# TensorE's inflows of a state-space scan, two states at a time in 64x128 tiles, with other steps left to VectorE

## The reference

```python
u, z = split(x @ in_w.T, 2)               # 256 channels each
u = silu(causal_conv(u))                  # 4 taps
dbc = u @ xproj_w.T                       # 64 for dt, 16 for B, 16 for C
dt = softplus(dbc[..., :64] @ dt_w.T + dt_b)
dA = exp(dt[..., None] * A)               # 16 states n
dBu = (dt * u)[..., None] * Bm[:, :, None, :]
h = dA_t * h + dBu_t                      # over the tokens t, for each channel and state
y = einsum('bdn,bn->bd', h, C_t) + u * D
out = y * silu(z) @ out_w.T
```

## Time and profile before

| | |
|---|---|
| median of 3 runs | 1566.91 us (1558.56 to 1570.34) |
| the profiled execution | 1558.44 us, span 1556.6 |
| Mamba stage in it | from about 10 to 975 us, a unit of it 58 |
| busy over the whole span | TensorE 87%, VectorE 75%, GpSimd 68%, ScalarE 62% |
| granted TensorE clock | 0.975 of full, 1.00 in most of the stage |
| chain that ended last | TensorE 52%, ScalarE 15%, VectorE 15%, GpSimd 5% |

### The profile page before, as it was taken

How to read it: one execution, slowest core, us unless ns; L and a number is a source line. 1 busy time by engine, 2 the same in 40 slices (tenths; PEclk the granted TensorE clock), 3 DMA queues, 4 the chain that set the end, 5 groups by cost and what they waited for, 6 DMA issues and landing times.

```text
span 1556.6 us, 43543 instructions
## 1 busy us (share of the span) xinstructions
PE 1347.9 (87%) x17914; PEld 1014.4 (65%) x17914; DVE 1161.2 (75%) x1926; ACT 958.4 (62%) x1750; POOL 1060.3 (68%) x684
## 2 busy tenths in 40 slices
PE   6798888889889989889889777898998999997595
PEld 3566766656756666666666666457997666666594
DVE  6788888888898887888888886523335888876376
ACT  6877777777766776876876765313555555542144
POOL 3798888888898888888888886340333466583552
PEclk9899999999999999999999989999999999999798
DMA  5122232232232222222222220531124200001223
GB/s 189 58 93 95 85 107 81 85 108 80 85 103 80 91 102 80 91 102 80 95 98 79 97 91 29 213 98 36 52 79 126 98 1 2 2 29 54 80 64 98
DMA packets 51604, 128.95 MB, mean 83 GB/s; under 512 B 8080, under 2 KB 33168, under 8 KB 41696
## 3 DMA queue, kind: packets, MB, share of 16 engines
q1 hardware_dynamic: 46640, 116.36, 21.8%
q0 software_dynamic: 4768, 9.81, 1.9%
HBM read 113.20 MB, written 18.56 MB: 85 GB/s over the span
## 4 chain that ended last, share of the span: by engine, by line
PE 52%; ACT 15%; DVE 15%; issue 8%; POOL 5%; another core or an unknown queue 2%; DMA 1%; SPq 1%; DVEq 0%; ACTq 0%; POOLq 0%
PE py L530 8%; PE pa L508 8%; DVE hh L925 5%; ACT da L723 4%; POOL hc L1077 3%; PE pr L1990 2%; PE bank L1536 2%; PE bank L1532 2%; PE bank L1546 2%; PE pq L413 2%; PE pq L385 2%; PE pr L2004 2%; ACT uz L625 2%; DVE hh L902 2%; PE pr L2193 2%
## 5 line engine op out<-in xcount | busy, mean ns | idle before, releaser
L1077 POOL TENSOR_TENSOR hc<-hh,cs 128x1024 f32<-128x1024 f32 x256 | 602.9, 2363 | 138.5 <-DVE hh L925 70.6
L925 DVE TENSOR_TENSOR_SCAN hh<-da,st,pa 128x512 f32<-128x512 f32 x240 | 293.6, 1266 | 65.5 <-PE pa L508 55.5
L508 PEld LDWEIGHTS pa<-dg,dtut 64*64 64x64 f32 x10240 | 180.8, 137 | 179.4 <-issue 175.6
L530 PE MATMUL py<-ident,hc 128*128 128x128 f32 x2048 | 277.1, 279 | 19.3 <-ACT yt L743 19.2
L508 PE MATMUL pa<-dg,dtut 64*64 64x64 f32 x10240 | 219.1, 226 | 80.9 <-DVE yz L934 38.5
L530 PEld LDWEIGHTS py<-ident,hc 128*128 128x128 f32 x2048 | 227.8, 142 | 44.7 <-ACT yt L743 21.2
L723 ACT ACTIVATE da<-dt,w 128x512 f32<-128x512 f32 x320 | 212.7, 711 | 11.3 <-DVE hh L925 10.4
L723 ACT ACTIVATE pa<-dt,w 128x512 f32<-128x512 f32 x192 | 127.7, 684 | 97.2 <-DVE hh L925 96.4
L925 DVE TENSOR_TENSOR_SCAN hh<-pa,st,hh 128x512 f32<-128x512 f32 x144 | 175.4, 1267 | 2.6 <-ACT pa L723 1.9
L385 PE MATMUL pq<-xn,w 128*128 128x512 f32 x248 | 121.0, 613 | 5.0 <-ACT xn L759 3.6
L925 DVE TENSOR_TENSOR_SCAN hh<-da,pa 128x512 f32<-128x512 f32 x80 | 93.2, 1207 | 29.4 <-PE pa L508 26.3
(11 more groups left out here) (349 smaller groups left out, 2807.8 us busy)
## 6 DMA issues: line engine op xcount, KB each, us to landing
cs<-bcrows SPq DMA_DIRECT2D x64, 1024.0 KB, 4.7
bs<-bcrows SPq DMA_DIRECT2D x32, 256.0 KB, 3.9
xsorted<-in_pads SPq DMA_DIRECT2D x13, 387.0 KB, 5.3
rot<-in_rot SPq DMA_DIRECT2D x4, 1024.0 KB, 5.0
wx<-in_l_w SPq DMA_DIRECT2D x4, 1024.0 KB, 10.3
ysort<-ytoken SPq DMA_DIRECT2D x14, 256.0 KB
wx<-in_l_w SPq DMA_DIRECT2D x1, 3072.0 KB, 12.3
wx<-in_l_w SPq DMA_DIRECT2D x1, 2304.0 KB, 16.7
```

Of the source, the lines that this page charges most:

```text
L508: i = pe.matmul(pa[turn["step", s, h] % SLOTS][c * HQ:(c + 1) * HQ, kt * P + r * HQ:kt * P + (r + 1) * HQ], dtut[rows, kt, h * P + c * HQ: ...
L530: i = pe.matmul(py[:, h * CH + kt * P:h * CH + (kt + 1) * P], hc[s % HCS][:, h, t], ident[:, :], is_transpose=True, start=n == 0 and kt == ...
L925: v.tensor_tensor_scan(hh[s % HHS][:, h, :], a, b, 0.0 if first else st[:, m % 2, n, h:h + 1], ALU.mult, ALU.add).then_inc(s_taken, 1)
L1077: g.tensor_tensor(hc[s % HCS][:, :, :], hh[s % HHS][:, :, :], cs[j % 2][:, s % CG, :].unsqueeze(1).broadcast_to([P, HF, CH]), ALU.mult).th ...
```

## The change

- `BY_G` is gone: GpSimd makes no inflow, the B rows are no longer loaded for it. `BY_V` becomes (6, 7, 12, 13), and TensorE has twelve steps: 0 to 5, 8 to 11, 14, 15.
- TensorE's steps go in pairs of states. The first step of a pair makes the inflows of both states for half 0, the second for half 1. VectorE scans accordingly two states for one half, and GpSimd's `times_c` and `keep_state` of either state wait for the second step; `keep_state` is done two steps later instead of one.
- An inflow is one block of 8 matmuls in 64x128 tiles: 64 tokens by 128 channels stationary, a diagonal of 64 for each of two states moving (128 columns). Rows 0 to 63 of the array write one bank of a pair, rows 64 to 127 the other. The two states are interleaved element by element over the pair, and the 128-token blocks by fours of tokens; a scan reads every second element of both banks. For that, `turn_b` and `turn_dtu` take every fourth token.
- A bank that held such an inflow is free only when both scans of its pair have read it (`free`).
- The order on TensorE changes: the inflow of step s + 1 first, then the spread, then `add_up`; in n = 10 it comes last.

```diff
-BY_G = (0, 12)
-BY_V = (1, 6, 11, 13)
-BY_P = tuple(n for n in range(NS) if n not in BY_G + BY_V)
+BY_V = (6, 7, 12, 13)
+BY_P = tuple(n for n in range(NS) if n not in BY_V)
...
-                pa = [bank(k, f"pa{i}") for i in range(SLOTS)]
+                pa2 = [bank(k, f"pa{i}", 2) for i in range(SLOTS // 2)]
+                pa = [pa2[i // 2][:, i % 2 * CH:(i % 2 + 1) * CH] for i in range(SLOTS)]
...
-                        order += [("step", s, h) for h in range(HF)]
+                        if n in BY_P:
+                            order += [("flow", pair_of(s), BY_P.index(n) % 2, j) for j in range(2)]
+                        else:
+                            order += [("step", s, h) for h in range(HF)]
...
+                def free(i):
+
+                    i -= SLOTS
+                    return i // 2 * 2 + 2 if handed_items[i][0] == "flow" else i + 1
+
+                def scanned(s):
+
+                    k = s % NS
+                    return (turn["flow", pair_of(s), HF - 1, BY_P.index(k) % 2] if k in BY_P else turn["step", s, HF - 1]) + 1
...
+                def by_fours(t):
+
+                    return t.rearrange("p (j k) -> p k j", k=4)
...
-                            i = pe.transpose(pb[:, kt * P:(kt + 1) * P], dtu[m % 2][:, h, kt * P:(kt + 1) * P], ident[:, :])
+                            i = pe.transpose(pb[:, kt * P:(kt + 1) * P], by_fours(dtu[m % 2][:, h, :])[:, kt, :], ident[:, :])
...
+                    def inflow(s):
+
+                        m, k, h = s // NS, pair_of(s), BY_P.index(s % NS) % 2
+                        i = turn["flow", k, h, 0]
+                        pe.wait_ge(s_turnk, turned_count(m, 2))
+                        pe.wait_ge(s_dg, k + 1)
+                        if i >= SLOTS:
+                            pe.wait_ge(s_taken, free(i + 1))
                         for kt in range(4):
                             for r in range(2):
-                                h, rows = (r + phase) % 2, slice(r * HQ, (r + 1) * HQ)
-                                for c in range(2):
-                                    i = pe.matmul(pa[turn["step", s, h] % SLOTS][c * HQ:(c + 1) * HQ, kt * P + r * HQ:kt * P + (r + 1) * HQ],
-                                                  dtut[rows, kt, h * P + c * HQ:h * P + (c + 1) * HQ], dg[pair % DGS][rows, of, kt, :],
-                                                  start=True, stop=True)
-                        i.then_inc(s_pin, 1)
+                                rows = slice(r * HQ, (r + 1) * HQ)
+                                mm = pe.matmul(pa[i % SLOTS + r].rearrange("p (j k n) -> p k n j", n=2, k=4)[:, kt, :, :],
+                                               dtut[rows, kt, h * P:(h + 1) * P], dg[k % DGS][rows, :, kt, :], start=True, stop=True)
+                        mm.then_inc(s_pin, 1)
...
-                        spreads = s + 2 < STEPS and by_vector(s + 2)
-                        if spreads and n != LAG:
+                        if s + 1 < STEPS and by_pe(s + 1) and n != 10:
+                            inflow(s + 1)
+                        if s + 2 < STEPS and by_vector(s + 2):
                             spread_b(s + 2)
...
-                        if flows:
-                            inflow(s + 1, 0)
...
                         if n != LAG and s >= LAG:
                             add_up(s - LAG)
-                        if flows:
-                            inflow(s + 1, 1)
...
                         prep(m + 1, n)
+                        if n == 10:
+                            inflow(s + 1)
...
+                        if by_pe(s):
+                            k, h = pair_of(s), BY_P.index(n) % 2
+                            for j in range(2):
+                                q = 4 * k + 2 * h + j
+                                if q >= DAS:
+                                    k0, j0 = (q - DAS) // 4, (q - DAS) % 4
+                                    act.wait_ge(s_taken, turn["flow", k0, j0 // 2, j0 % 2] + 1)
...
-                        if s >= 1:
-                            keep_state(s - 1)
+                        if s >= 2:
+                            keep_state(s - 2)
...
+                        if by_pe(s):
+                            k, h = pair_of(s), BY_P.index(n) % 2
+                            own = PAIRS[k % len(PAIRS)]
+                            if h == 0 and NS * m + own[1] >= HHS:
+                                v.wait_ge(s_hc, NS * m + own[1] - HHS + 1)
+                                v.wait_ge(s_st, kept_states(NS * m + own[1] - HHS))
+                            v.wait_ge(s_pin, 2 * k + h + 1)
+                            for j, nj in enumerate(own):
+                                i, q = turn["flow", k, h, j], 4 * k + 2 * h + j
+                                v.wait_ge(s_slot, slot_count(i))
+                                inflows = pa2[i // 2 % (SLOTS // 2)][:, j::2]
+                                v.tensor_tensor_scan(hh[(NS * m + nj) % HHS][:, h, :], da[q % DAS][:, :], inflows,
+                                                     0.0 if first else st[:, m % 2, nj, h:h + 1], ALU.mult, ALU.add).then_inc(s_taken, 1)
```

More of the change, by code:

```diff
@@ L217, in layer0_mamba @@
             s_crow, s_cout = sem("bc_rows_kept"), sem("bc_rows_out")
-            s_cin, s_bin = [sem(f"c_in{i}") for i in range(2)], sem("b_in")
+            s_cin = [sem(f"c_in{i}") for i in range(2)]
             s_hc, s_st = sem("hc_made"), sem("state_kept")
@@ L747, in keep_state @@
                             return
-                        act.wait_ge(s_taken, turn["step", s, HF - 1] + 1)
+                        act.wait_ge(s_taken, scanned(s))
                         act.activation(st[:, s // NS % 2, s % NS, :], hh[s % HHS][:, :, CH - 1], ACT.Identity).then_inc(s_st, 1)
@@ L918, in scan @@
                             v.wait_ge(s_st, kept_states(NS * (m - 1) - 1))
-                        for h in range(HF):
-                            i = turn["step", s, h]
-                            v.wait_ge(s_slot, slot_count(i))
-                            a, b = pa[i % SLOTS][:, :], hh[s % HHS][:, h, :]
-                            if by_pe(s):
-                                a, b = da[2 * (before(BY_P, s) % 2) + h][:, :], pa[i % SLOTS][:, :]
-                            v.tensor_tensor_scan(hh[s % HHS][:, h, :], a, b,
-                                                 0.0 if first else st[:, m % 2, n, h:h + 1], ALU.mult, ALU.add).then_inc(s_taken, 1)
+                        if by_pe(s):
[11 more added lines that the diff above has]
+                                                     0.0 if first else st[:, m % 2, nj, h:h + 1], ALU.mult, ALU.add).then_inc(s_taken, 1)
+                        else:
+                            v.wait_ge(s_db, made(BY_V, s))
+                            for h in range(HF):
+                                i = turn["step", s, h]
+                                v.wait_ge(s_slot, slot_count(i))
+                                v.tensor_tensor_scan(hh[s % HHS][:, h, :], pa[i % SLOTS][:, :], hh[s % HHS][:, h, :],
+                                                     0.0 if first else st[:, m % 2, n, h:h + 1], ALU.mult, ALU.add).then_inc(s_taken, 1)
                     def gate(m):
@@ L1063, in b_diagonals @@
                         if k >= DGS:
-                            m0, last = (k - DGS) // len(PAIRS), PAIRS[(k - DGS) % len(PAIRS)][-1]
-                            g.wait_ge(s_pin, 2 * before(BY_P, NS * m0 + last) + 2)
-                        columns = bt[m % 2][:, :, own[0]:own[-1] + 1:own[-1] - own[0]].rearrange("p t n -> p n t")
+                            g.wait_ge(s_pin, 2 * (k - DGS) + 2)
+                        columns = bt[m % 2][:, :, own[0]:own[1] + 1].rearrange("p t n -> p n t")
                         g.tensor_tensor(dg[k % DGS][:, :, :, :], eye2[:, :].unsqueeze(1).unsqueeze(1).broadcast_to([P, 2, 4, HQ]),
@@ L1070, in times_c @@
                     def times_c(s):
-                        g.wait_ge(s_taken, turn["step", s, HF - 1] + 1)
+                        g.wait_ge(s_taken, scanned(s))
                         j = s // CG
@@ L1086, in mamba_gpsimd @@
                     g.wait_ge(s_small, 96)
-                    inflow(0)
-                    b_diagonals(0)
+                    for k in range(2):
+                        b_diagonals(k)
                     for s in range(STEPS):
@@ L1092, in mamba_gpsimd @@
                             dt_times_u(m + 1)
-                        if s + 2 < STEPS and (s + 2) % NS in BY_G:
-                            inflow(s + 2)
-                        ahead = [k for k in range(1, UNITS * len(PAIRS)) if NS * (k // len(PAIRS)) + PAIRS[k % len(PAIRS)][0] == s + 4]
+                        ahead = [k for k in range(2, UNITS * len(PAIRS)) if NS * (k // len(PAIRS)) + PAIRS[k % len(PAIRS)][0] == s + 4]
                         for k in ahead:
```

91 lines of the change are left out of this document (25 added, 66 removed).

## The result

The changed kernel takes 1614.35 us (1611.34 to 1618.21), the kernel before 1563.87 beside it (four runs, one more than before the forecast): ratio 1.032, 95% interval 1.027 to 1.037. The forecast was 1585. So the sign was right and the size was not: +50 us instead of +18.

A forecast was written before the change was run, and what follows sets the result against it. Handovers bound each unit: TensorE's queue in pieces 1, 2 and 4, VectorE in piece 3. 0.9 + 0.35 + 1.13 - 1.1 = +1.28 us a unit, +18 us in all, on the median 1566.9 gives 1585; range 1545 to 1615.

The forecast's parts named there:

- The mechanism: State-space stage: no engine is full; handovers set a unit's length, TensorE's queue in three pieces, VectorE in the other.
- piece 1: From the scan of step 0 to the end of the gate: 19.8 us before, forecast +0.9 through TensorE's queue.
- piece 3: From the first `factor` to the scan of step 13: 9.5 us before, forecast +1.13 for one more VectorE inflow.
- Piece 4: From the scan of step 13 to the next unit's scan 0: 11.1 us before, forecast 10.0, so -1.1.
- The block: TensorE's 8 matmuls in two passes for a whole step's inflow: taken as 1.05 us from three estimates, 1.02 to 1.09.
- Estimate (a): Price of a TensorE block as twice an old phase plus the switch of tile shape: 1.09 us.
- the price of 0.15 for entering: TensorE's `add_up` ahead of an inflow takes 1.03 us against 0.87 ahead of anything else, so entering costs 0.15 more.
- Piece 2: From the end of the gate to the first `factor`: 17.5 us before, forecast 17.8, so +0.35.
- the strided output: Rival: blocks writing columns 32 bytes apart double the column time, a block 1.92 us, 1715 in all; chance 0.10.
- the dtu transposes: Rival: transposes reading every fourth element of dtu take twice 0.5 us a group, +15 us, 1600; chance 0.13.
- the switches: Rival: TensorE's row tiles lose the 0.3 us tile-shape switches, saving 45 us, 1540; chance 0.14, half for a part.
- nothing: Rival: the bare wait and the extra inflow are worth as much as the queue gains, 1567; chance 0.16.

The follow-up runs named there:

- no_dd: Changed kernel without the 16 matmul instructions a unit that add u * D to y: ratio 1.0225 to the kernel before.
- fill_uz3: Changed kernel with four unread 512-column matmuls a unit added in TensorE's pauses and three `uz` tiles instead of two: ratio 1.019 to the kernel before.
- fill: Changed kernel with four 512-column matmuls a unit, whose products nobody reads, added in TensorE's pauses: ratio 1.023 to the kernel before.
- flat_out: Changed kernel with each matmul of a block writing its 128 columns to adjacent places instead of 32 bytes apart: ratio 1.035 to the kernel before.
- v1: Changed kernel with one of VectorE's four inflows moved from step 7 to step 1: ratio 1.006 to the kernel before.
- uz3: Changed kernel with three `uz` tiles instead of two: ratio 1.0385 to the kernel before.

## Why the prediction was right or wrong

- *The mechanism*: right in the main. TensorE's queue sets piece 1 up to scan 4 (`no_dd`, `fill_uz3`) and, by the timelines, pieces 2 and 4; VectorE sets piece 3. GpSimd binds nowhere: in the changed kernel it is busy 46.0 us of 62 instead of 49.6 of 58, and between 400 and 900 us VectorE is not seen to wait for it. The engine that was missing is ScalarE: in piece 1 VectorE waits for its exponentials, in the changed kernel 1.67 us.
- *Piece 3*, +1.13: measured +1.04. *Piece 4*, -1.1: measured -0.8, with 2.15 us of idle ahead of scan 0 where about 2 was expected. The queue came as counted; scan 0 starts 1.40 us after the start of block 0 (403.31 to 404.71) where 1.15 was put down.
- *The block*, 1.05: mis-sized, 1.10. Estimate (a), twice a phase and one switch, was right with 1.09; it was averaged with two weaker ones. Ten blocks on the path make 0.45 us a unit.
- *Into and out of a block*: the price of 0.15 for entering came from `add_up` groups with a phase on either side. An `add_up` only ahead of a block takes 0.96 to the next start, one only behind it 0.93, one with neither 0.87; so it is 0.09 in and 0.06 out. A group of u * D behind a block takes 0.99 (404.40 to 405.39) instead of 0.89, which was not counted. In piece 1 these errors cancel: from block 0 to block 4 the queue takes 12.9 us, 12.7 were forecast, and the four blocks make the difference.
- *Piece 1*, +0.9: mis-sized. It was counted for TensorE and VectorE alone. The third engine's wait was missed, the silu for the `add_up` of step 12. In the kernel before that `add_up` was done just in time (the silu's table load did not wait), and scan 3 stood 0.69 us for ScalarE. It makes 0.5 us a unit (`fill_uz3` against `fill`).
- *Piece 2*, +0.35: the step that failed most, +2.4 in the long units and +0.9 at the full clock. The start of block 8 was right (5.27 after the gate, 5.2 forecast). But the text counted the pause only as a delay, and did not ask what TensorE's clock would do after 6.5 us of pauses in 12. The halved clock costs 0.7 us a unit (`fill`). The forecast took every price from rows at 1.00. At the full clock, in `fill`, block 8 to the end of `out_project` takes 10.6 us instead of 10.1: 0.15 are the blocks, and 0.23 the four small transposes of B (`turn_b`), which take 0.59 to the next start behind an `add_up` (430.98 to 431.57) where they took 0.36 behind a phase (414.94 to 415.30 before). They also read every fourth token now; no run separates the two causes.
- *Sum*: of the 1.9 us a unit beyond the forecast's 1.3, the clock is 0.7 (`fill`) and the silu's wait 0.5 (`fill_uz3`), both by experiment. The 0.7 by which `fill_uz3` (59.92) is above the forecast's 59.2 is what is left over, so the sum closes by construction; the blocks are 0.45 of it, and the rest goes by the rows above, without an experiment of its own. 14 units give 45.0 of the 57.5 us by which the two profiled spans differ; the last unit gives 3.4, and 9 lie behind the stage, where the changed kernel's own two executions differ by 37.
- *The rivals*: the strided output costs nothing (`flat_out`); the dtu transposes take 0.48 a group, as before; the switches did not go away, a block still has about 0.2 beyond its columns; "nothing" fell.
- *What the forecast did not separate*: that the change is a gain of 1.35 us a unit and a loss of 4.6. It never asked whether other places for VectorE's four steps would cost less; `v1` shows that 2.1 us of a unit at the full clock (`fill` against it) hang on one of them.

## What to carry to other kernels

When work moves between engines in a hand-written order, cost the place as well as the engine: a step that needs nothing from the queue that sets the pace is worth most in the middle of a run of steps that do, and an instruction that waits for a shared ring or bank costs all that is queued behind it. For each engine outside the pair that is being compared, list the waits that the kernel before satisfied just in time. If the forecast opens pauses in TensorE, price the work behind them at either clock, and test the parts of a change apart: here the tiles alone would have been a gain. Waits that are taken away one at a time can move the lowered clock onto work that pays for it, as three `uz` tiles did; so read the clock of every test kernel too.

## What the runs showed of the hardware

- The granted clock fell to 0.50 once in nearly every unit of the changed kernel, in which TensorE pauses 6.5 us in 12: in the long units behind the third pause, on a block that then took 2.01 us instead of 1.10, in the short ones behind the first. Matmuls whose product nobody reads, 4 us a unit, kept it at 1.00 and made the kernel 1.2% faster. The kernel before, with pauses of 1.07 and 2.85 us there, had 1.00.
- Which work pays for it shifts with the length of a unit: the same changed kernel has units of 60.6 and 62.2 us, and in `uz3` nearly all are at 61.2 to 61.8, with three of 64.5. So a wait taken away (0.5 us a unit at the full clock) made the kernel no faster.
- fp32 matmuls that write 128 columns 32 bytes apart in PSUM take as long as with adjacent columns, 1.09 us a block; scans that read every second element of PSUM take 1.26 us, as before.
- A group of eight 128-column fp32 matmul instructions on the full array takes 0.87 us to the next start, 0.96 ahead of a block of 64x128 row tiles, 0.93 behind one and 1.02 between two.
